# First attention: the causal mask added by TensorE, VectorE takes a plain row maximum

## What is computed

```python
x = _layernorm(x)                       # 4 x 512 x 256
q, k, v = (split_heads(x @ W.T) for W in (Wq, Wk, Wv))   # 16 heads of 16
sim = einsum('bhsd,bhtd->bhst', q, k) * scale
sim = where(causal, sim, -inf)
weights = softmax(sim, axis=-1)
out = einsum('bhst,bhtd->bhsd', weights, v)
```

## Time and profile before

| | |
|---|---|
| median of 3 runs | 1226.99 us (1226.29 to 1227.85) |
| the profiled execution | 1226.03 us, span 1224.3 us |
| TensorE matmuls busy | 1167.3 us (95%), weight loads 1004.5 us |
| VectorE busy | 895.2 us (73%) |
| ScalarE busy | 692.3 us (57%) |
| GpSimd busy | 580.1 us (47%) |
| custom maximum, L1135, both attentions | 512 times, 235.3 us |

### The profile page before, as it was taken

One profiled execution on the slowest core, in us unless ns is written; L12 is line 12 of the kernel. 1 busy time (PEld: TensorE's weight loads), 2 busy tenths in 40 slices (PEclk: granted clock), 3 DMA queues, 4 the chain that ended last, 5 costly groups with the idle time before them and its releaser, 6 DMA issues.

```text
span 1224.3 us, 25085 instructions
## 1 busy us (share of the span) xinstructions
PE 1167.3 (95%) x7980; PEld 1004.5 (82%) x7980; DVE 895.2 (73%) x2799; ACT 692.3 (57%) x1717; POOL 580.1 (47%) x844
## 2 busy tenths in 40 slices
PE   6999999899999999999999999999998889999994
PEld 5766566689999999999999999999997769999961
DVE  5777888577777777887777887778876755555555
ACT  3487888655556565556564565655566434444432
POOL 4063655454344444447353365534354446666650
PEclk9999999999999999999999999999999989999998
DMA  8965655355631121212112132111214137777776
GB/s 264 286 184 170 178 164 176 91 178 175 204 109 62 57 84 57 80 52 91 68 36 69 36 102 73 43 63 35 70 62 134 61 114 122 117 119 118 111 143 206
DMA packets 111715, 139.58 MB, mean 114 GB/s; under 512 B 11300, under 2 KB 94756, under 8 KB 111460
## 3 DMA queue, kind: packets, MB, share of 16 engines
q1 hardware_dynamic: 97140, 119.10, 32.1%
q0 software_dynamic: 14448, 18.88, 9.6%
HBM read 63.36 MB, written 61.87 MB: 102 GB/s over the span
## 4 chain that ended last, share of the span: by engine, by line
PE 79%; DVE 6%; ACT 3%; POOL 3%; issue 3%; DMA 3%; SPq 2%; POOLq 0%; ACTq 0%; DVEq 0%
PE bank L1513 59%; PE bank L1755 6%; PE bank L1932 4%; PE bank L1574 2%; PE bank L1627 2%; PE bank L1610 2%; PE bank L1617 1%; POOL xs_rows L704 1%; DMA sum_rows<-mid,goal 1%; POOL sum_rows L766 1%; PE bank L1911 1%; PE bank L1942 1%; SPq L393 1%; DVE bank L1135 1%; ACT pT L862 1%
## 5 line engine op out<-in xcount | busy, mean ns | idle before, releaser
L1135 DVE CUSTOM_DVE_ANT_0 bank<-bank,mask 128x512 f32<-128x512 f32 (+3 forms) x512 | 235.3, 522 | 40.4 <-PE bank L1610 20.4
L970 ACT ACTIVATE p<-bank,stat 128x512 f32<-128x512 f32 (+3 forms) x256 | 131.4, 526 | 137.9 <-issue 133.2
L557 POOL CAST w_hl<-raw_qkv 128x512 fp32r<-128x512 f32 x96 | 58.5, 610 | 313.3 <-DMA raw_qkv<-in_qkvo 159.6
L1513 PE MATMUL bank<-xT,w_hl 128*128 128x512 f32 x768 | 189.6, 395 | 0.0
L1513 PEld LDWEIGHTS bank<-xT,w_hl 128*128 128x128 f32 x768 | 144.1, 188 | 34.6
L766 POOL DMA_INDIRECT sum_rows<-mid,goal x79 | 123.1, 1559 | 75.4 <-DVE mid L1468 64.3
L1513 PE MATMUL bank<-pT,v 128*128 128x128 f32 (+3 forms) x768 | 137.3, 328 | 0.0
L1234 DVE SCALAR_TENSOR_TENSOR qk<-bank,qk 128x512 fp32r<-128x512 f32 x128 | 87.1, 688 | 66.8 <-ACT qk L910 66.5
L1513 PE MATMUL bank<-qk 128*128 128x512 f32 (+3 forms) x768 | 130.8, 320 | 3.1 <-DVE pT L1345 2.4
L1513 PEld LDWEIGHTS bank<-qk 128*128 128x128 f32 x768 | 120.6, 191 | 12.2 <-DVE v L1234 2.6
L558 POOL TENSOR_TENSOR w_hl<-raw_qkv,w_hl 128x512 fp32r<-128x512 f32 x96 | 124.0, 1292 | 7.8
(11 more groups left out here) (237 smaller groups left out, 2284.6 us busy)
## 6 DMA issues: line engine op xcount, KB each, us to landing
raw_qkv<-in_qkvo SPq DMA_DIRECT2D x32, 768.0 KB, 5.6
xs_rows<-blank SPq DMA_DIRECT2D x32, 520.0 KB, 3.5
xs_rows<-blank SPq DMA_DIRECT2D x5, 2730.0 KB, 14.0
xrow<-xs_rows SPq DMA_DIRECT2D x79, 130.0 KB, 2.5
raw_o<-in_qkvo SPq DMA_DIRECT2D x32, 256.0 KB, 3.8
sum_rows<-blank SPq DMA_DIRECT2D x3, 2176.0 KB, 8.5
stk<-xT SPq DMA_DIRECT2D x96, 64.0 KB
stk<-k_hl SPq DMA_DIRECT2D x96, 64.0 KB
```

Source lines behind the costliest of these rows:

```text
L970: act.activation(p2[:, n % 2, POFF[qi]:POFF[qi + 1]], s2(t), ACT.Exp, scale=-1.0, bias=stat2[:, 0, n % 2, t:t + 1], accum_out=stat2[:, 1, ...
L1135: return dve.tensor_tensor_reduce(scores, scores, mask[:, TB - scores.shape[1]:], scale=-1.0, scalar=-2.0 * MASKED, op0=ALU.add, op1=ALU.m ...
L1513: ins = pe.matmul(out, a, b, start=start and i == 0, stop=stop and i == len(pairs) - 1, **kw)
```

## The change

In the first attention the mask is no longer added by VectorE. Behind each score, or each pair of blocks that share a bank, TensorE adds a product of a 16-bit identity (128 x 128) with the last 128 columns of the 16-bit mask to the 128 columns on the diagonal (`forbid`): six such products for a pair of heads, four of 128 columns and two of 256. The score leaves its accumulation open, and the first of two blocks in one bank alone clears the bank's marks. VectorE's `row_max` is a plain `tensor_reduce` with max, which writes nothing but its column of `least`. The maxima are therefore not negated, and the row of 1 in `stk` becomes -1. GpSimd makes the 16-bit identity at the start, and TensorE waits for it. Everything else, the second attention included, is the same.

```diff
--- before.py
+++ after.py
@@ -87,6 +87,7 @@
         xT = sb(ctx, "xT", [P, B, 2, C, TB], F32R)
         ident = sb(ctx, "ident", [P, P])
 
+        ident16 = sb(ctx, "ident16", [P, P], BF16)
         mask = sb(ctx, "mask", [P, TB], BF16)
         ln_w = sb(ctx, "ln_w", [P, 2, C])
         gate_raw = sb(ctx, "gate_raw", [P, C, E])
@@ -505,7 +506,8 @@
                                base=0, pattern=[[-1, P]], channel_multiplier=1).then_inc(const, 1)
             pool.wait_ge(const, 4)
             pool.tensor_copy(mask[:, :], mask_f).then_inc(const, 1)
-            pool.wait_ge(const, 5)
+            pool.tensor_copy(ident16[:, :], ident[:, :]).then_inc(const, 1)
+            pool.wait_ge(const, 6)
             pool.memset(blank[:, :], 0.0).then_inc(d_blank, 1)
             pool.wait_ge(d_blank, 1)
             pool.iota(blank[:, D:D + 1].bitcast(I32), [[0, 1]], base=NOWHERE, channel_multiplier=0)\
@@ -513,7 +515,7 @@
             pool.memset(f32(stk[:, :, :, :]), 0.0).then_inc(stk_zero, 1)
             for a in range(2):
                 pool.wait_ge(stk_zero, 1 + a)
-                pool.memset(f32(stk[64 * a:64 * a + 1, :, 1, :]), 1.0).then_inc(stk_zero, 1)
+                pool.memset(f32(stk[64 * a:64 * a + 1, :, 1, :]), -1.0).then_inc(stk_zero, 1)
             pool.wait_ge(stk_zero, 3)
             pool.wait_ge(ph1_wl, 1)
             pool.tensor_tensor(qkv1_hl[:, LO, :, 2 * D:3 * D], qkv1[:, :, 2 * D:3 * D],
@@ -1180,7 +1182,7 @@
                 def row_max(a, *sizes):
 
                     for n in sizes:
-                        ins = mask_and_max(s1(a, n), least[:, (s + 1) % 2, n - 1, 64 * a:64 * a + 1])
+                        ins = dve.tensor_reduce(least[:, (s + 1) % 2, n - 1, 64 * a:64 * a + 1], s1(a, n), AX.X, ALU.max)
                     ins.then_inc(a1_max, 1)
 
                 def weigh(i):
@@ -1513,7 +1515,7 @@
                     ins = pe.matmul(out, a, b, start=start and i == 0, stop=stop and i == len(pairs) - 1, **kw)
                 return ins
 
-            pe.wait_ge(const, 5)
+            pe.wait_ge(const, 6)
             def turn_x(b):
                 pe.wait_ge(ph1_xn, b * TPB + TPB)
                 if b:
@@ -1524,6 +1526,13 @@
                                            ident[:, :])
                     ins.then_inc(ph1_tp, 1)
 
+            def forbid(a, *sizes):
+
+                own = s1(a, sizes[0])[:, P * (sizes[0] - 1):P * sizes[0]] if len(sizes) == 1 else \
+                    bank[a][:, 2 * P:4 * P].rearrange("p (i n) -> p i n", i=2)
+                future = mask[:, TB - P:] if len(sizes) == 1 else mask[:, TB - P:].unsqueeze(1).to_broadcast([P, 2, P])
+                return pe.matmul(own, ident16[:, :], future, start=False, stop=True, skip_group_check=True)
+
             def first_scores():
 
                 pe.wait_ge(stk_in[0], 16 * 7)
@@ -1532,7 +1541,8 @@
                         pe.wait_ge(ph1_lo, 4 * (B - 1) + 1)
                     rows = slice(64 * a, 64 * a + 64)
                     pe.matmul(s1(a, n), stk[rows, 0, 0, P * (n - 1):P * n], stk[rows, 0, 1, 0:P * n],
-                              start=True, stop=True).then_inc(a1_s, 1)
+                              start=True, stop=False, skip_group_check=True)
+                    forbid(a, n).then_inc(a1_s, 1)
 
             turn_x(0)
             for b in range(B):
@@ -1608,7 +1618,7 @@
 
                     rows, m, qi = slice(64 * a, 64 * a + 64), r % NSTK, n - 1
                     return pe.matmul(s1(a, n), stk[rows, m, 0, P * qi:P * (qi + 1)], stk[rows, m, 1, 0:P * n],
-                                     start=True, stop=True)
+                                     start=n > 1, stop=False, skip_group_check=True)
 
                 def score_t(a, n):
 
@@ -1634,7 +1644,8 @@
                     pe.wait_ge(stk_in[r % NSTK], 16 * 7 * (r // NSTK + 1))
                     for i, (a, n) in enumerate(S1_PARTS):
                         pe.wait_ge(a1_max, 6 * (r - 1) + i + 4)
-                        score(r, a, n).then_inc(a1_s, 1)
+                        score(r, a, n)
+                        forbid(a, n).then_inc(a1_s, 1)
                 if 0 <= s < N1:
 
                     if s >= 1:
@@ -1677,11 +1688,12 @@
                     for a, n in S1_REST:
                         if n == 3:
                             pe.wait_ge(a1_max, 6 * r + 1 + a)
-                        ins = score(r, a, n)
+                        score(r, a, n)
                         if n == 1:
-                            ins.then_inc(a1_s, 1)
+                            forbid(a, 3, 1).then_inc(a1_s, 1)
                     pe.wait_ge(a1_max, 6 * r + 3)
-                    score(r, 1, 2).then_inc(a1_s, 1)
+                    score(r, 1, 2)
+                    forbid(1, 2).then_inc(a1_s, 1)
                 if 0 <= s < N1:
                     pe.wait_ge(a1_m, 2 * (s + 1))
                     for i, (a, n) in enumerate(S1_PARTS):
```

## The result

The changed kernel takes 1284.74 us (median of 5 runs, 1269.38 to 1288.01) against 1226.99 before: 4.5% slower, ratio 1.0447, 95% interval 1.0409 to 1.0485. Five runs of before (the three of the table and two more beside the changed kernel) lie within 2.4 us of one another, those of the changed kernel within 18.6. The profiled execution took 1277.85 us, 51.8 more than the profiled one of before.

The account below looks back on a forecast made before the run. TensorE was taken to bound the first attention, mostly waiting for nobody, with array shape changes costing time: 72 us added, less 16 covered by waits, is 56 on 1226.0, so 1282 us; range 1262 to 1308.

Parts of the forecast that it names:

- the cover: First attention: of TensorE's 27 us of waits, 16 are real and all hide added TensorE work.
- Emptying the array at a change of shape: TensorE, first attention: each shape change empties the array; the next burst starts 0.07 us before the last matmul's end.
- Prices of the bursts: TensorE, first attention: product 0.23 us for 128 columns, 0.29 for 256; top group 1.73, rest group 1.68.
- the gross of 72 us: TensorE, first attention: +2.28 us a step, 70.7 over 31 steps, plus about 1.6 for the first pair.
- the lower end: First attention: the full 27 us of TensorE's waits hide added work, giving the low side of the forecast.
- rival 3: First attention: sparser TensorE work drops the clock to half; half the stage so gives +60, 1340 us; chance 0.06.
- VectorE's part at nothing beside TensorE's: First attention: VectorE's gain of 0.5 us a step (0 to 1.1) counts 0, as TensorE makes it wait.
- The bound of 0.06 us for an operation: VectorE, first attention: a plain maximum gains some 0.06 us over the custom operation, between 0 and 0.14.
- rival 4: First attention: VectorE becomes the bound, needing 7 us a step instead of 4.4; chance left within Rival 1.
- Rival 2: First attention: products stream without emptying the array, 0.44 us a step, 14 us, held by waits; 1220 us; chance 0.04.
- Rival 1: First attention: nothing is covered and a product costs as much as the f32 transpose; 91 us, 1317; chance 0.09.
- GpSimd's conversion and the wait at the start: Kernel start: one 128x128 conversion on GpSimd, about 0.2 us, far from the stage, costs nothing.

Follow-up runs that it names:

- the dense start: Changed kernel plus eight 512-column products into an unread bank at the start of each of the stage's first two steps: 1276.70 us, ratio 1.0414.
- VectorE's half alone: Kernel before with plain row maximum, no mask ahead of it, row of -1, TensorE as before: 1223.72 us, ratio 0.9975; second set 1223.13 us.

## Why the prediction was right, and where it was not

*Side and range.* Forecast 1282, range 1262 to 1308; measured 1284.7. The nearness of the two is in part luck, since two errors of 9 and 11 us, the cover and the clock, cancel.

*Emptying the array at a change of shape* held term by term. The 0.07 us before the end of the burst ahead stand at every product shown. The Trainium skill (TensorEngine Tiling, Key Properties) says that changing the tiling mode drains the TensorE; the runs agree: 57.7 us for the whole change, 2.5 with the products in the scores' shape.

*Prices of the bursts.* Product of 128 columns: taken 0.23, measured 0.23; of 256: taken 0.29, measured 0.28. Rest group: taken 1.68, measured 160.12-158.47 = 1.65. Top group: taken 1.73; from its first product to its end 1.29 measured, against 1.73-0.50+0.07 = 1.30. So the gross of 72 us stands.

*The cover* was the term mis-sized: taken 16 us, measured 25. In the same 28 steps, all at full clock, the transposes of the maxima (one group a step) stand here, before and after:

```profile
73.15 0.33 PE L1574 MATMUL bank<-ident,least 128*128 128x128 f32 x1 [0.20 <-ACT pT L862]
...
224.40 0.33 PE L1574 MATMUL bank<-ident,least 128*128 128x128 f32 x1 [0.48 <-ACT pT L862]
```

```profile
82.51 0.28 PE L1584 MATMUL bank<-ident,least 128*128 128x128 f32 x1
...
275.04 0.33 PE L1584 MATMUL bank<-ident,least 128*128 128x128 f32 x1 [0.48 <-ACT pT L864]
```

That is 192.5 us against 151.3, +1.47 a step: 46 over 31 steps, and 47 with the 1.6 of the first pair, where the bursts alone come to 72. The line of the runs says the same: at the 32 us of half clock of before it gives 1274, 47 over 1227. So 72-47 = 25 us were covered, near the 27 of the lower end. I had taken 0.17 us off each of 62 waits as emptying. But counted in the trace, 26 of these 62 stand between two loads of one shape (as the one at 57.60 in the earlier trace rows), where nothing is emptied. The weight loads' waits account for 27.1-8.3 = 19 of the 25; where the other 6 lie the rows don't separate.

*The clock* (rival 3, 0.06) came true in part, beside the forecast instead of in its place, and the sign named for it, a clock under 1.00 after 70 us, stands in the windows. The median run spent 59 us at half clock, 27 more than before; at 0.41 each, 11 us. 47+11 = 58, the measured 57.7. That work at the start of the stage decides is borne out by the dense start; that fewer columns per us are the reason, as the rival had it, is not shown. Its price (a step of 11 us for 7) was about right: with the custom operation, steps that take 6.0 and 6.6 us at full clock took 9.9 and 10.9 at half. The objection to it misread: the routed experts have 126 matmuls in 20.00 us that are all busy, 6.3 a us, and the start of the stage 43 in 7 us, 6.1 a us. They are not far between, so their clock of 1.00 said nothing against the rival.

*VectorE's part at nothing beside TensorE's* was right (0.1 us in the mean with the custom operation back, at equal time at half clock). The bound of 0.06 us for an operation fits too:

```profile
L1185 DVE TENSOR_REDUCE least<-bank 128x1 f32<-128x512 f32 x61 | 39.3, 684 | 40.7 <-PE bank L1534 40.7
...
L1185 DVE TENSOR_REDUCE least<-bank 128x1 f32<-128x128 f32 x62 | 17.4, 281 | 0.0
```

And before:

```profile
L1135 DVE CUSTOM_DVE_ANT_0 bank<-bank,mask 128x512 f32<-128x512 f32 x62 | 41.8, 714 | 9.6 <-PE bank L1610 9.5
```

684 ns against 714, and 281 against 330, and alone it is worth 3.5 us. That VectorE would idle some 60 us more came out (87.3-27.3), in part by luck, since the stage's 50.2 us hold what the clock cost; it also rules out rival 4. What it waits for now, and before:

```profile
DVE least L1185 <- PE bank L1534: 63.2, 39, 3.5
```

```profile
DVE bank L1135 <- PE bank L1610: 19.5, 27, 1.9
```

*Rival 2* (the products stream, 1220) describes the kernel with products in the scores' shape. It came to 1229.8, not 1220, some 6 us over VectorE's half alone, so even then TensorE's added 14 us were not wholly covered. *Rival 1* is out: a product takes 0.23 us, and most waits are gone. *GpSimd's conversion and the wait at the start* left no trace: the first transposes of the stage stand at 58.3 where they stood at 57.9, and the mask products of the first pair lie ahead of that.

## What to carry to other kernels

On an engine whose work is a chain of short matmuls, count the changes of array shape before counting columns: here a product that streams for 0.06 to 0.11 us cost 72/186 = 0.39 us of TensorE's time where it parted two bursts of another shape, 47/186 = 0.25 after what waits could cover. If such work must be added, put it in the shape of its neighbours, or in one group. And ask first whether it is needed: the maximum did not need the mask at all, and leaving it out was the only version that gained, 3.5 us or 0.3%.

## What the runs showed of the hardware that was not expected

The clock can stay at half under a TensorE that is busy without a gap. In the changed kernel it fell at 64.3 us, after a stretch of single bursts with a busy share of 5.76 in 6.00 us, and stayed down through 17.1 us whose matmul rows are busy 17.10; in the kernel with the custom operation through 58.0 us. A burst of one takes 0.27 us beside the 0.055 for every 128 columns (the prices of the earlier trace rows), so a busy row is not one of streaming. At half clock a group of scores and products takes about half as long again (92.67+0.29-90.38 = 2.58 us for 1.65). What lets it rise again, in mid-stage and with the work unchanged, is open. The Trainium skill (TensorE: Matmul & The Clock Gate, HAM oscillation) ties a lost clock to idle gaps between matmuls. Here the gaps in the rows come to 0.24 us in the 6.00 us ahead of the fall and to none in the 17.1 us at half clock, so the measurement decides. The cost is 0.41 us for each us spent at half clock.
